# A factorization-machine kernel with attention: the order of its first loads, one gather source for all rows, and later places for transposes, grams and masks

## The chip, the cores and the metric

One core of a Trainium2 chip runs the kernel. The metric is the time of one execution on the device in microseconds; the time before is the median of three runs. Engines are TensorE (PE), VectorE (DVE), ScalarE (ACT), GpSimd (POOL) and SyncE (SP). SP and ACT each feed a DMA queue of their own, and GpSimd feeds a third one.

## The reference

For each of 2048 batch elements, 32 integer indices pick 32 rows of an embedding table (12500 x 64, fp32). Every pair of the 32 rows is multiplied element by element, put through a small attention layer, and summed with the attention score as weight.

```
V = emb_v[x]                                  # (32, 2048, 64); x is brought into 0..12499
iu, ju = np.triu_indices(32, k=1)             # 496 pairs
VV = V[iu] * V[ju]
hid = relu(einsum('pbk,kh->pbh', VV, at_w) + at_b)
score = einsum('pbh,ho->pbo', hid, at_h)
at_fm_score = sum(VV * score, axis=0) @ p
logit = at_fm_score + w0 + sum(w1[x], axis=0)
prob = sigmoid(logit)
```

Since p is applied after the sum over pairs, `VV @ p` of a pair (i, j) is an entry of a weighted Gram matrix of the 32 rows of one batch element. The kernel computes that matrix ("gram"), computes the scores of all pairs, and multiplies the two.

## The kernel before

The batch is cut into 32 **fills** of 64 elements each. A fill's rows come by 16 indirect DMAs of 128 rows each, issued by GpSimd (`gather`, L262), into one of two buffers `rows`. On PE, eight transposes (`turn`, L504) put them into a slot of the PSUM tensor `Z`; ACT copies them to `V` (`keep_v`, L418), scales them by p in two halves (`keep_pv`, L427) and copies the w1 column out (`keep_w1`, L438). A fill then has 16 **rounds** (`ORDER`). In a round, DVE makes products of pairs, `X` (L409); PE multiplies them by `at_w` into `Z` (`hidden`, L536); ACT applies bias and relu, giving `H` (L489). `X` and `H` have four slots of two rounds each, `Z` has three slots of one round, and the transposes take a turn of one of the three. After rounds 3, 7, 11 and 15 PE computes the scores of two steps (`scores`, L553), those after round 3 for the fill before. `grams` (L570) is 128 small matmuls. DVE masks a gram (`mask_gram`), multiplies it by the scores (`weigh`) and sums the pairs (`sum_pairs`).

Each engine's order is written out by hand. Before the change, the transposes of fill t+1 stand ahead of round 8 of fill t, and the grams of fill t+1 stand at the end of fill t. Fill 0 and the last fill are written out; the 30 between are a hardware loop of 15 turns, two fills in each (`over_fills`, L199). The end of a turn is thus the end of every second fill, where each engine jumps back.

**The joint table.** A gathered row should bring its w1 value along. So the kernel first builds a table in DRAM with 66 values a row: it loads the whole embedding table in four pieces of 768 KB (`load_piece`, two on SP's queue, two on ACT's) and w1; DVE and ACT copy both into `joined`, and `store_piece` writes it back. The last 212 rows go through `tail` and `tail_w1`. Gathers from the table wait until everything of it is stored (L286). To start sooner, the eight gathers of the first half of fill 0 read the raw embedding table instead, and eight more at the very end fetch their w1 values (L302). DVE brings the indices into range first (L313 to L321). Small operands (p, bias, hcol, at_w in two halves each, w0) are loaded through SP's queue between the table's loads and its stores.

Gathers of fill t from 4 on are paced by waits on PE's progress: on `scored`, and on `z_ready` by `GROUP_AFTER`.

## Time and profile before

| what | us |
|---|---|
| median of 3 runs | 851.7 |
| lowest, highest run | 846.13, 852.37 |
| profiled execution, its own time | 846.66 |
| its span in the profile | 844.6 |
| PE busy in the span | 785.1 |
| DVE, ACT, POOL busy | 701.3, 648.1, 549.0 |

The span runs from the first to the last recorded instruction; the execution's own time is 2.06 us longer. Busy is the time in which an engine had an instruction running; waits and the issuing of DMAs by SP and ACT are not in it. The chain that ended last is followed back from the last instruction to whatever released each step, so its shares say where the end was decided.

### The profile page before, as it was taken

The page shows a single profiled execution, that of the slowest core. Times are in us where ns is not written, and L with a number is a line of the kernel's source. Part 1 is how long each engine was busy: PE and PEld are TensorE (multiplying, and loading weights), DVE is VectorE, ACT ScalarE, POOL GpSimd, SP SyncE. Part 2 cuts the span into 40 slices and gives each one's busy share as a digit, 9 for nine tenths or more (in the row PEclk, how much of TensorE's full clock was granted, in tenths as well). Part 3 has the DMA queues.
Part 4 walks back from the last instruction along what each step waited for, and adds up shares of the span by engine and source line. Part 5 has one row for each costly group of instructions (what it writes and reads, how often), then busy time and mean ns, then how long its engine had stood idle before and what let it go on. Part 6 is the DMA issues. An engine that isn't in the chain of part 4 may idle for free.

```text
span 844.6 us, 30455 instructions
## 1 busy us (share of the span) xinstructions
PE 785.1 (93%) x12600; PEld 336.8 (40%) x12600; DVE 701.3 (83%) x1181; ACT 648.1 (77%) x679; POOL 549.0 (65%) x530
## 2 busy tenths in 40 slices
PE   0368799999999999999999999999999999999998
PEld 0123344444434444444344444434444444344443
DVE  3367788889988888899888889998888899888883
ACT  2256577878888788888878888887878788887885
POOL 4377776666677666666776666667766666767500
PEclk9979899999999999999999999999999999999999
DMA  7458887532424436333233436352322436323100
GB/s 238 107 26 26 25 25 26 22 22 22 22 23 23 21 21 23 21 22 23 22 23 22 22 21 22 22 25 20 23 22 21 22 21 23 24 20 23 9 1 2
DMA packets 19138, 24.20 MB, mean 29 GB/s; under 512 B 9705, under 2 KB 9774, under 8 KB 19118
## 3 DMA queue, kind: packets, MB, share of 16 engines
q0 software_dynamic: 16640, 17.07, 39.5%
q1 hardware_dynamic: 1703, 3.61, 1.1%
q10 hardware_dynamic: 774, 3.25, 1.0%
q8 instruction: 13, 0.21, 0.1%
q14 instruction: 8, 0.06, 0.0%
HBM read 20.59 MB, written 3.31 MB: 28 GB/s over the span
## 4 chain that ended last, share of the span: by engine, by line
PE 83%; POOL 4%; issue 4%; DVE 3%; DMA 3%; SPq 2%; ACT 0%; DVEq 0%; POOLq 0%
PE Z L549 50%; PE SG L564 26%; POOL rows L276 4%; PE SG L579 4%; PE Z L513 4%; DVE X L409 3%; DMA table<-joined 1%; DMA rows<-table,joint_idx 1%; SPq L236 1%; PE Z L634 0%; SPq L237 0%; SPq L229 0%; SPq L239 0%; SPq L238 0%; DVE part L384 0%
## 5 line engine op out<-in xcount | busy, mean ns | idle before, releaser
L276 POOL DMA_INDIRECT rows<-table,joint_idx x504 | 531.0, 1054 | 233.9 <-issue 144.9
L409 DVE TENSOR_TENSOR X<-V 128x992 f32<-128x992 f32 (+15 forms) x1024 | 635.9, 692 | 40.9 <-PE Z L549 22.0
L489 ACT ACTIVATE H<-Z,bias 128x1024 f32<-128x1024 f32 x512 | 536.6, 1118 | 112.5 <-PE Z L549 109.2
L549 PE MATMUL Z<-X,w_sb 64*64 64x512 f32 x4096 | 473.6, 598 | 9.2 <-issue 5.1
L549 PEld LDWEIGHTS Z<-X,w_sb 64*64 64x64 f32 x4096 | 153.0, 133 | 242.4 <-issue 237.4
L564 PE MATMUL SG<-H,score_w 128*32 128x496 f32 (+15 forms) x4096 | 248.4, 382 | 0.0
L564 PEld LDWEIGHTS SG<-H,score_w 128*32 128x32 f32 x4096 | 109.4, 110 | 204.0 <-issue 109.5
L435 ACT ACTIVATE pV<-V,pmask 128x1024 f32<-128x1024 f32 x64 | 81.0, 1269 | 0.1
L378 DVE TENSOR_TENSOR prod<-SG,gram 128x496 f32<-128x496 f32 x32 | 21.6, 674 | 67.5 <-PE SG L564 67.5
L424 ACT COPY V<-Z 128x1024 f32<-128x1024 f32 x31 | 31.4, 1014 | 43.0 <-PE Z L513 43.0
L579 PE MATMUL SG<-V,pV 128*32 128x32 f32 x4096 | 43.7, 198 | 3.2 <-ACT pV L435 1.6
L579 PEld LDWEIGHTS SG<-V,pV 128*32 128x32 f32 x4096 | 43.1, 109 | 7.1 <-issue 3.8
L513 PE MATMUL Z<-ident,rows 128*128 128x128 f32 x248 | 34.7, 284 | 5.8 <-DMA rows<-table,joint_idx 5.8
L525 PE MATMUL SG<-ident,rows 128*128 128x128 f32 x8 | 2.2, 428 | 38.7 <-DMA rows<-in_L_rec_emb_v_dram,idx 29.9
L513 PEld LDWEIGHTS Z<-ident,rows 128*128 128x128 f32 x248 | 27.3, 143 | 8.7 <-DMA rows<-table,joint_idx 5.0
L370 DVE TENSOR_TENSOR gram<-SG,upper 128x496 f32<-128x496 f32 x32 | 21.6, 675 | 9.8 <-PE SG L579 8.2
L384 DVE TENSOR_REDUCE part<-prod 128x496 f32 (+1 forms) x32 | 21.1, 660 | 0.0
L525 PEld LDWEIGHTS SG<-ident,rows 128*128 128x128 f32 x8 | 1.4, 216 | 39.5 <-issue 29.9
L276 POOL DMA_INDIRECT rows<-in_L_rec_emb_v_dram,idx x8 | 9.3, 1168 | 10.4 <-DVE idx L317 8.3
L358 DVE COPY score_w<-hcol 64x1 f32<-64x1 f32 x32 | 2.2, 150 | 10.3 <-DMA w_sb<-in_L_rec_w_dram 10.3
L443 ACT COPY w_all<-rows 128x8 f32 (+2 forms) x64 | 10.4, 227 | 0.0
L463 ACT COPY V<-SG 128x512 f32<-128x512 f32 x2 | 1.2, 587 | 12.1 <-PE SG L525 12.1
(42 smaller groups left out, 31.9 us busy)
## 6 DMA issues: line engine op xcount, KB each, us to landing
rows<-table,joint_idx POOLq DMA_INDIRECT x504, 3.7
table<-joined ACTq DMA_DIRECT2D x2, 792.0 KB
table<-joined SPq DMA_DIRECT2D x2, 792.0 KB
raw<-in_L_rec_emb_v_dram ACTq DMA_DIRECT2D x2, 768.0 KB, 6.7
raw<-in_L_rec_emb_v_dram SPq DMA_DIRECT2D x2, 768.0 KB, 9.1
idx_raw<-in_r_x_dram SPq DMA_DIRECT2D x4, 64.0 KB, 5.9
rows<-in_L_rec_emb_v_dram,idx POOLq DMA_INDIRECT x8, 6.6
w_all<-in_L_rec_w_dram,idx POOLq DMA_INDIRECT x8
```

The source lines that it names most:

```text
L276: pool.indirect_dma_start(out=rows[t % 2][:, g * FILL_M + m, half, c0:c1], out_offset=None, in_=source, in_offset=bass.IndirectOffsetOnAxi ...
L370: nc.vector.tensor_tensor(gram[parity][:, :, 1:FIELDS], SG[parity][:, :, 1:FIELDS], upper[:, 1:FIELDS].unsqueeze(1).to_broadcast(shape), A ...
L378: nc.vector.tensor_tensor(prod[:, :, 1:FIELDS], SG[parity][:, :, 1:FIELDS], gram[parity][:, :, 1:FIELDS], ALU.mult).then_inc(prod_ready, 1)
L384: nc.vector.tensor_reduce(part[:, bass.ds(t * GROUP, GROUP)], prod[:, :, 1:FIELDS], AX.X, ALU.add).then_inc(part_ready, 1)
L409: last_one = nc.vector.tensor_tensor(xo, vj, vi.unsqueeze(3).to_broadcast(shape), ALU.mult)
L424: nc.scalar.copy(V[parity][:, :, :], Z[:, TURN_SLOT, :, :].rearrange("p g (b f) -> p (g b) f", f=FIELDS)).then_inc(v_ready, 1)
L435: nc.scalar.activation(pV[:, :, half, :, :], V[parity][:, :, :].rearrange("p b (i c) -> p b c i", c=2), ACT.Copy, scale=pmask[:, half:half ...
L489: nc.scalar.activation(H[:, s % H_SLOTS, :, COLS * g:COLS * g + COLS], Z[:, z_slot(r), :, :], ACT.Relu, bias=bias[:, 0:1]).then_inc(hid_re ...
L513: last = nc.tensor.transpose(Z[:, TURN_SLOT, g, 128 * m:128 * m + 128], embs[:, g * FILL_M + m, 1:1 + 2 * EMB], ident[:, :])
L549: done = nc.tensor.matmul(Z[64 * par:64 * par + 64, z_slot(r), half, :], w_sb[k, :], X[k, s % X_SLOTS, par, COLS * g:COLS * g + COLS], sta ...
L564: last = nc.tensor.matmul(SG[parity][at:at + 32, :, j0:FIELDS], score_w[:, slot, :], hid.rearrange("p (b j) -> p b j", j=nj), start=(s == ...
L579: last = nc.tensor.matmul(SG[parity][at:at + 32, b, :], pV[:, g * GROUP + b, half, :, :].rearrange("p c i -> p (c i)"), V[parity][:, g * G ...
```

## The change

Nine things are altered:
- SP loads its two table pieces ahead of the indices; ACT loads w1 ahead of its two pieces.
- The tail's rows, the tail of w1 and all nine small loads are issued by GpSimd, which also joins the tail (two copies) and stores it.
- DVE joins w1 and its two table pieces ahead of the work on the indices.
- All 16 gathers of fill 0 read the joint table and wait for it. The early gathers from the raw table, the zeroing of their w1 column, and the eight w1 gathers at the end are gone.
- The transposes of the next fill stand ahead of round 12 instead of 8; ACT's copy to `V` moves with them, and `keep_w1` is ahead of round 14.
- `grams(t)` stands in its own fill t, behind the scores after round 3; ACT makes its two `pV` halves ahead of rounds 0 and 2 of that fill.
- DVE masks ahead of round 10, weighs ahead of 11, sums ahead of 13 (before: 8, 10, 12).
- The gathers' pacing waits are later: `scored` by two steps, `GROUP_AFTER` (0, 6, 10, 13).
- `turn(1)` keeps its old slot of `Z` by a name of its own.

```diff
@@ -43,13 +43,15 @@
-TURN_BEFORE = 8
+TURN_BEFORE = 12
+PV_BEFORE = (0, 2)
+MASKED_BEFORE, WEIGHED_BEFORE, SUMMED_BEFORE = 10, 11, 13
 SCORED_AFTER = {3: (-1, (6, 7)), 7: (0, (0, 1)), 11: (0, (2, 3)), 15: (0, (4, 5))}
 LAST_STEPS = (6, 7)
 X_SLOTS, H_SLOTS, Z_SLOTS = 4, 4, 3
 ROW = EMB + 1
-EMB_AT, W1_AT = (1, 0), (0, EMB)
+W1_AT = (0, EMB)
 JOINT = EMB + 2
@@ -57,7 +59,7 @@
 TAIL = (VOCAB - MAIN) // TAIL_RUN
-GROUP_AFTER = (0, 3, 7, 10)
+GROUP_AFTER = (0, 6, 10, 13)
@@ -71,7 +73,7 @@
-TURN_SLOT = TURN_BEFORE % Z_SLOTS
+TURN_SLOT, FIRST_TURN_SLOT = TURN_BEFORE % Z_SLOTS, Z_SLOTS - 1
@@ -225,22 +227,12 @@
+            for k in range(PIECES // 2):
+                load_piece(sp, k)
             for q in range(QUARTERS):
                 sp.dma_start(idx_raw[q * FIELDS:(q + 1) * FIELDS, :],
                              r_x[:, q * NB:(q + 1) * NB]).then_inc(idx_loaded, 16)
-            for k in range(PIECES // 2):
-                load_piece(sp, k)
-            sp.dma_start(tail[:, :, 1:1 + EMB], last_rows(emb_v)).then_inc(tail_loaded, 16)
-            for half in range(2):
-                lo, hi = half * 64, half * 64 + 64
-                sp.dma_start(pcol[lo:hi, :], p).then_inc(small_loaded, 16)
-                sp.dma_start(bias[lo:hi, :], at_b.rearrange("(h o) -> h o", o=1)).then_inc(small_loaded, 16)
-                sp.dma_start(hcol[lo:hi, :], at_h).then_inc(small_loaded, 16)
-                sp.dma_start(w_sb[lo:hi, :], at_w).then_inc(small_loaded, 16)
-            sp.dma_start(w0_sb[:, :], w0.to_broadcast([QUARTERS, 1])).then_inc(small_loaded, 16)
-            sp.wait_ge(w1_joined, 4)
-            sp.wait_ge(tail_loaded, 16)
-            sp.dma_start(last_rows(table), tail[:, :, :]).then_inc(table_stored, 16)
+            sp.wait_ge(w1_joined, 2)
             for k in range(PIECES // 2):
@@ -264,27 +256,34 @@
                         if paced and g == 0 and m == 0:
-                            pool.wait_ge(scored, STEPS * (t - 3) + LAST_STEPS[0] - 1)
+                            pool.wait_ge(scored, STEPS * (t - 3) + LAST_STEPS[0] + 1)
                         elif paced and m % 2 == 0:
                             pool.wait_ge(z_ready, ROUNDS * (t - 2) + GROUP_AFTER[2 * g + m // 2])
-                        joint = t > 0 or g > 0
-                        source, at_rows = (flat, joint_idx) if joint else (emb_v, idx)
                         for half in range(2):
                             col = (2 * half + g) * NM + t * FILL_M + m
-                            c0, c1 = (0, ROW) if joint else (EMB_AT[half], EMB_AT[half] + EMB)
                             arrived = first_rows[g] if t == 0 else second_rows if t == 1 else rows_gathered[t % 2]
-                            pool.indirect_dma_start(out=rows[t % 2][:, g * FILL_M + m, half, c0:c1], out_offset=None,
-                                                    in_=source,
-                                                    in_offset=bass.IndirectOffsetOnAxis(ap=at_rows[:, col:col + 1], axis=0)
+                            pool.indirect_dma_start(out=rows[t % 2][:, g * FILL_M + m, half, :], out_offset=None, in_=flat,
+                                                    in_offset=bass.IndirectOffsetOnAxis(ap=joint_idx[:, col:col + 1], axis=0)
                                                     ).then_inc(arrived, 16)
+            pool.dma_start(tail[:, :, 1:1 + EMB], last_rows(emb_v)).then_inc(tail_loaded, 16)
+            pool.dma_start(tail_w1[:, :], w1[MAIN:VOCAB, :].rearrange("(p r) o -> p (r o)", r=TAIL_RUN)).then_inc(tail_loaded, 16)
             for half in range(2):
-                nc.gpsimd.memset(rows[0][:, 0:FILL_M, half, W1_AT[half]], 0.0).then_inc(w1_cleared, 1)
-            pool.wait_ge(idx_ready, 1)
-            gather(0, groups=(0,))
+                lo, hi = half * 64, half * 64 + 64
+                pool.dma_start(hcol[lo:hi, :], at_h).then_inc(small_loaded, 16)
+                pool.dma_start(pcol[lo:hi, :], p).then_inc(small_loaded, 16)
+                pool.dma_start(bias[lo:hi, :], at_b.rearrange("(h o) -> h o", o=1)).then_inc(small_loaded, 16)
+                pool.dma_start(w_sb[lo:hi, :], at_w).then_inc(small_loaded, 16)
+            pool.dma_start(w0_sb[:, :], w0.to_broadcast([QUARTERS, 1])).then_inc(small_loaded, 16)
+            pool.wait_ge(tail_loaded, 32)
+            for c in (0, 1 + EMB):
+                nc.gpsimd.tensor_copy(tail[:, :, c], tail_w1[:, :]).then_inc(tail_joined, 1)
+            pool.wait_ge(tail_joined, 2)
+            pool.dma_start(last_rows(table), tail[:, :, :]).then_inc(tail_stored, 16)
             pool.wait_ge(idx_ready, 4)
-            pool.wait_ge(table_stored, 16 * (PIECES + 1))
-            gather(0, groups=(1,))
+            pool.wait_ge(table_stored, 16 * PIECES)
+            pool.wait_ge(tail_stored, 16)
+            gather(0)
             gather(1)
@@ -296,16 +295,18 @@
                 gather(t, paced=True)
-            for half in range(2):
-                for n in range(FILL_M):
-                    at = bass.IndirectOffsetOnAxis(ap=idx[:, 2 * half * NM + n:2 * half * NM + n + 1], axis=0)
-                    pool.indirect_dma_start(out=w1_all[:, 2 * half, n:n + 1], out_offset=None, in_=w1, in_offset=at
-                                            ).then_inc(w1_first, 16)
         @block.vector
         def _(dve):
+            dve.wait_ge(w1_loaded, 16)
+            for c in (0, 1 + EMB):
+                nc.vector.tensor_copy(joined[:, :, c], raw_w1[:, :]).then_inc(w1_joined, 1)
+            for k in range(PIECES // 2):
+                dve.wait_ge(raw_loaded[k], 16)
+                r0, r1 = k * PIECE, (k + 1) * PIECE
+                nc.vector.tensor_copy(joined[:, r0:r1, 1:1 + EMB], raw[:, r0:r1, :]).then_inc(rows_joined[k], 1)
             dve.wait_ge(idx_loaded, 16 * QUARTERS)
@@ -390,11 +383,11 @@
                         dve.wait_ge(first_v, g + 1)
-                    if r == 8:
+                    if r == MASKED_BEFORE:
                         mask_gram(t, parity)
-                    if r == 10 and not first:
+                    if r == WEIGHED_BEFORE and not first:
                         weigh(t - 1, 1 - parity)
-                    if r == 12 and not first:
+                    if r == SUMMED_BEFORE and not first:
                         sum_pairs(t - 1)
@@ -421,7 +414,8 @@
                     act.wait_ge(gram_ready, t - 1)
-                nc.scalar.copy(V[parity][:, :, :], Z[:, TURN_SLOT, :, :].rearrange("p g (b f) -> p (g b) f", f=FIELDS)
+                slot = FIRST_TURN_SLOT if isinstance(t, int) and t == 1 else TURN_SLOT
+                nc.scalar.copy(V[parity][:, :, :], Z[:, slot, :, :].rearrange("p g (b f) -> p (g b) f", f=FIELDS)
                                ).then_inc(v_ready, 1)
@@ -437,17 +431,15 @@
-                g0 = 1 if isinstance(t, int) and t == 0 else 0
                 for half in range(2):
-                    src = rows[parity][:, :, half, W1_AT[half]].rearrange("p (g m) -> p g m", g=2)[:, g0:2, :]
-                    nc.scalar.copy(w1_all[:, 2 * half + g0:2 * half + 2, bass.ds(t * FILL_M, FILL_M)], src
+                    src = rows[parity][:, :, half, W1_AT[half]].rearrange("p (g m) -> p g m", g=2)
+                    nc.scalar.copy(w1_all[:, 2 * half:2 * half + 2, bass.ds(t * FILL_M, FILL_M)], src
                                    ).then_inc(w1_kept, 1)
+            nc.scalar.dma_start(raw_w1[:, :], w1[0:MAIN, :].rearrange("(p r) o -> p (r o)", p=128)).then_inc(w1_loaded, 16)
             for k in range(PIECES // 2, PIECES):
                 load_piece(nc.scalar, k)
-            nc.scalar.dma_start(raw_w1[:, :], w1[0:MAIN, :].rearrange("(p r) o -> p (r o)", p=128)).then_inc(w1_loaded, 16)
-            nc.scalar.dma_start(tail_w1[:, :], w1[MAIN:VOCAB, :].rearrange("(p r) o -> p (r o)", r=TAIL_RUN)).then_inc(w1_loaded, 16)
-            act.wait_ge(w1_joined, 3)
+            act.wait_ge(w1_joined, 2)
             for k in range(PIECES // 2, PIECES):
@@ -467,14 +458,12 @@
                     if not last and not first:
-                        if r == 8:
+                        if r == TURN_BEFORE:
                             keep_v(t + 1, 1 - parity)
-                        if r == 10:
-                            keep_pv(t + 1, 1 - parity, 0)
-                        if r == 12:
+                        if r == 14:
                             keep_w1(t + 1, 1 - parity)
-                        if r == 14:
-                            keep_pv(t + 1, 1 - parity, 1)
+                    if not first and r in PV_BEFORE:
+                        keep_pv(t, parity, PV_BEFORE.index(r))
                     if first and r == STEPS // 2:
@@ -490,8 +479,6 @@
                     keep_v(1, 1)
-                    for half in range(2):
-                        keep_pv(1, 1, half)
                     keep_w1(1, 1)
@@ -507,10 +494,11 @@
                     pe.wait_ge(rows_gathered[parity], gathered(t, parity))
+                slot = FIRST_TURN_SLOT if isinstance(t, int) and t == 1 else TURN_SLOT
                 embs = rows[parity][:, :, :, :].rearrange("p t h k -> p t (h k)")
                 for g in range(2):
                     for m in range(FILL_M):
-                        last = nc.tensor.transpose(Z[:, TURN_SLOT, g, 128 * m:128 * m + 128],
+                        last = nc.tensor.transpose(Z[:, slot, g, 128 * m:128 * m + 128],
                                                    embs[:, g * FILL_M + m, 1:1 + 2 * EMB], ident[:, :])
@@ -608,12 +596,11 @@
                                 scores(t - 1, 1 - parity, s)
-                    if r == ROUNDS - 1 and not last:
-                        grams(t + 1, 1 - parity)
+                        if back < 0 and not first:
+                            grams(t, parity)
             def linear_term():
-                pe.wait_ge(w1_first, 16 * 2 * FILL_M)
                 pe.wait_ge(w1_kept, 2 * FILLS)
```

## Rows read from the trace of the kernel before

**Rows 1.** The page: busy time of each engine, its share of the span, instructions.

```profile
PE 785.1 (93%) x12600; PEld 336.8 (40%) x12600; DVE 701.3 (83%) x1181; ACT 648.1 (77%) x679; POOL 549.0 (65%) x530
```

**Rows 2.** Waits of the PE from 120 to 800 us: total, times, longest.

```profile
PE Z L549 <- issue: 5.1, 12, 0.5
PE Z L549 <- DVE X L409: 0.8, 2, 0.4
```

**Rows 3.** Timeline of the PE, two boundaries between fills: start, us, line, idle before.

```profile
156.97 1.31 PE L579 MATMUL SG<-V,pV 128*32 128x32 f32 x128
158.32 3.66 PE L549 MATMUL Z<-X,w_sb 64*64 64x512 f32 x32
...
179.35 1.94 PE L564 MATMUL SG<-H,score_w 128*32 128x368 f32 x32
181.10 1.31 PE L579 MATMUL SG<-V,pV 128*32 128x32 f32 x128
182.83 2.38 PE L549 MATMUL Z<-X,w_sb 64*64 64x512 f32 x20 [0.42 <-issue]
```

**Rows 4.** Timeline of the start, all engines and queues: start, us, line, idle before.

```profile
4.77 8.67 SPq L236 DMA_DIRECT2D pcol<-in_L_rec_p_dram  x1
...
12.94 0.26 DVE L327 COPY joined<-raw_w 128x96 f32<-128x96 f32 x1 [1.05 <-DMA tail_w<-in_L_rec_w_dram]
...
27.49 2.17 DVE L358 COPY score_w<-hcol 64x1 f32<-64x1 f32 x32 [10.31 <-DMA w_sb<-in_L_rec_w_dram]
```

**Rows 5.** The chain that ended last: start, us, what.

```profile
20.81 11.90 DMA table<-joined
```

**Rows 6.** Busy time by stretch, after the engines: granted clock, DMA share, GB/s.

```profile
22.00:24.00 2.00, 0.00 (x0) 0.00 (x0) 0.00 (x0) 0.00 (x0) 0.00 (x0) 1.00 0.75 63
...
26.00:28.00 2.00, 0.00 (x0) 0.00 (x0) 0.51 (x9) 0.20 (x1) 0.00 (x0) 1.00 0.96 362
```

**Rows 7.** Timeline of GpSimd: one early gather, then the 8th and 40th from the table.

```profile
12.81 2.45 POOL L276 DMA_INDIRECT rows<-in_L_rec_emb_v_dram,idx  x1 [0.30 <-issue]
...
42.74 0.94 POOL L276 DMA_INDIRECT rows<-table,joint_idx  x1 [0.30 <-issue]
...
83.92 0.95 POOL L276 DMA_INDIRECT rows<-table,joint_idx  x1 [0.30 <-issue]
```

**Rows 8.** Timeline of the PE, first, second and third fill.

```profile
29.89 1.08 PE L525 MATMUL SG<-ident,rows 128*128 128x128 f32 x4 [29.89 <-DMA rows<-in_L_rec_emb_v_dram,idx]
...
46.56 1.11 PE L525 MATMUL SG<-ident,rows 128*128 128x128 f32 x4 [8.76 <-DMA rows<-table,joint_idx]
...
69.16 1.07 PE L513 MATMUL Z<-ident,rows 128*128 128x128 f32 x8 [0.96 <-DMA rows<-table,joint_idx]
...
93.34 1.97 PE L513 MATMUL Z<-ident,rows 128*128 128x128 f32 x8 [4.86 <-DMA rows<-table,joint_idx]
95.24 4.83 PE L549 MATMUL Z<-X,w_sb 64*64 64x512 f32 x32
...
108.65 0.96 PE L579 MATMUL SG<-V,pV 128*32 128x32 f32 x64 [0.68 <-issue]
109.65 3.66 PE L549 MATMUL Z<-X,w_sb 64*64 64x512 f32 x32
```

**Rows 9.** Timeline of ScalarE in the third fill.

```profile
121.73 1.01 ACT L424 COPY V<-Z 128x1024 f32<-128x1024 f32 x1 [1.25 <-PE Z L513]
122.86 2.12 ACT L489 ACTIVATE H<-Z,bias 128x1024 f32<-128x1024 f32 x2
124.87 1.28 ACT L435 ACTIVATE pV<-V,pmask 128x1024 f32<-128x1024 f32 x1
```

**Rows 10.** The page: groups of products, of weighing and of w1 copies: count, busy, mean ns.

```profile
L409 DVE TENSOR_TENSOR X<-V 128x992 f32<-128x992 f32 (+15 forms) x1024 | 635.9, 692 | 40.9 <-PE Z L549 22.0
...
L378 DVE TENSOR_TENSOR prod<-SG,gram 128x496 f32<-128x496 f32 x32 | 21.6, 674 | 67.5 <-PE SG L564 67.5
...
L443 ACT COPY w_all<-rows 128x8 f32 (+2 forms) x64 | 10.4, 227 | 0.0
```

More of the change, by code:

```diff
@@ L163, in afm_kernel @@
         w1_joined = sem("w1_joined")
-        w1_cleared = sem("w1_cleared")
+        tail_joined = sem("tail_joined")
+        tail_stored = sem("tail_stored")
         table_stored = sem("table_stored")
@@ L173, in afm_kernel @@
         ident_ready = sem("ident_ready")
-        w1_first = sem("w1_first")
         first_rows = [sem(f"first_rows{g}") for g in range(2)]
@@ L322, in _ @@
                                         ).then_inc(idx_ready, 1)
-            dve.wait_ge(w1_loaded, 32)
-            for c in (0, 1 + EMB):
-                nc.vector.tensor_copy(joined[:, :, c], raw_w1[:, :]).then_inc(w1_joined, 1)
-                nc.vector.tensor_copy(tail[:, :, c], tail_w1[:, :]).then_inc(w1_joined, 1)
-            for k in range(PIECES // 2):
-                dve.wait_ge(raw_loaded[k], 16)
-                r0, r1 = k * PIECE, (k + 1) * PIECE
-                nc.vector.tensor_copy(joined[:, r0:r1, 1:1 + EMB], raw[:, r0:r1, :]).then_inc(rows_joined[k], 1)
             nc.vector.memset(zeros[:, :], 0.0)
@@ L457, in _ @@
             act.wait_ge(small_loaded, 16 * 9)
-            act.wait_ge(w1_cleared, 2)
             nc.scalar.activation(warm[:, :], w0_sb[:, :], ACT.Sigmoid).then_inc(sigmoid_loaded, 1)
```

## The prediction, made before the kernel with the change had run

> **What bounds it now.** I read the page's busy shares first: PE is busy 93% of the span, and no other engine is above 83% [rows 1]. Then the waits of PE between 120 and 800 us: 5.1 us in 12 gaps of kind "issue" and 0.8 in two more [rows 2]. In 680 us that is all, so from the third fill on PE sets the time, and work moved about on DVE, ACT or GpSimd is worth nothing there unless it makes PE wait. The timeline of PE shows where those gaps sit: at a boundary inside a loop turn, grams end at 158.28 and the next products follow at 158.32; where the loop jumps back, grams end at 182.41 and products start at 182.83 [rows 3]. Fills 1 to 30 are 15 turns, hence 14 jumps: 14 x 0.42 = 5.9 us.
>
> The rest of PE's idle time is at the start. First transposes 29.89, second group 46.56, those of fill 1 69.16, those of fill 2 93.34, products of fill 2 109.65 [rows 8]; three of the four ended a wait for gathered rows. The gathers waited for the table, whose last stores landed at 20.81 + 11.90 = 32.7 [rows 5]. I call that moment T.
>
> **Edit 1: the table earlier.** Before, SP's queue was held 8.67 us in issuing pcol and free at 13.44; w1, behind ACT's two pieces, reached DVE at 12.94 [rows 4]. So the loads end near 13, and they carry the same bytes after. What falls away is the time between 13 and 20.8, in which SP issued small loads. Pieces 0 and 2 will have landed early and be joined by then. Four stores of 792 KB are 3.24 MB; at 362 GB/s [rows 6] that is 9.0 us, so T is 22.0 at best. Before, the last two stores took 11.9 us for bytes worth 4.5, behind small loads that held the DMA engines at 0.75 share for 63 GB/s [rows 6]. At worst they do so again: 13 + 4.5 + 11.9 = 29.4. The small loads still use the same engines, only from another queue, earlier. I take 2.5 us for them: T = 24.5, nearer the lower end since the queue ahead of the stores is now empty.
>
> The tail goes through GpSimd: 11 loads, two copies, one store. No row shows a plain DMA from GpSimd. The nearest is a gather: from the 8th to the 40th, (83.92 - 42.74)/32 = 1.29 us each [rows 7]. From about 2: 11 x 1.29 = 14.2, copies at most 0.5, store 1.3, landing 2.9 (8th gather issued by 43.68, its rows used at 46.56). That is 21. One gather beside DVE's copies into the table took 2.45 instead of 0.94 [rows 7]; twice that excess gives 24, still under T. Lower end: an issue of 0.6, T unaffected. Upper end: every one at 2.45 + 0.3, T = 2 + 30.3 + 4.7 = 37. I take 1.29.
>
> Small operands were ready at 27.49 + 2.17 = 29.7 [rows 4] and bounded the first transposes; now those come at T + 13.8 = 38.3, which covers the loads, the index work after DVE's joins (under 3 us) and the constants. If that cover goes, they cost what they end beyond 38.3.
>
> **Edit 2: 48 gathers in one row.** Before, rows were there at T + 13.8 (8 gathers), T + 36.4 (24), T + 60.6 (40): (93.34 - 46.56)/32 = 1.46 us each, slower than their issue. Kept at 1.46: 16 gathers T + 25.5, 32 T + 48.9, 48 T + 72.3. Losing the early eight costs 8 x 1.46 = 11.7 us; that is the price of the single source. The eight w1 gathers at the end were on nobody's path: nothing.
>
> **Edit 3: what fill 1 does while it waits.** PE reached the transposes of fill 2 after eight rounds, waited 4.86 us, and still had eight rounds and the grams to do. After, it has twelve rounds done. From the transposes of fill 1: V 2.1, first X 1.25 (DVE needs 635.9/512 = 1.24 a round [rows 10]), four rounds at DVE's pace to 8.2, scores to 10.1, grams 1.3 plus a first-time gap of 0.68 [rows 8] to 12.1, four rounds 15.8, scores 17.7, four rounds 21.4, scores 23.3: T + 72.2. Rows come at T + 72.3, so PE hardly waits. Then transposes 1.0, four rounds 3.66, scores 1.94: fill 2 starts at T + 78.9. Its grams (1.3) now lie within it, so T + 80.2 stands against 109.65. The head gives T - 29.4; at T = 24.5 that is **-4.9 us**. Break-even is T = 29.4.
>
> **Edit 4: the loop's jump.** Ahead of the jump stood 128 grams in 1.31 us, 10 ns for a matmul with its weight load. Now it is 32 score matmuls in 1.94 us, 60 ns each [rows 3]. Whatever PE's sequencer has run ahead by is worth six times as much time. Gain between 0 and 5.9; I take all, as grams at 10 ns a pair were fed without a hole, so the queue should be full under scores. The Trainium skill, Advanced Engine Details and Errata, section Engine Queue Depths, gives TensorE a queue of 64; by it the scores cover nearly their whole 1.94 us. No run here shows the depth.
>
> **Edit 5: steady rounds.** Take a fill's first products as 0. Transposes end at -5.5, V is copied by -4.5 (1.01 [rows 9]). DVE then starts 4.5 us ahead instead of eight rounds ahead: X(3) at +0.5, wanted at 2.7; ten rounds, then the mask (0.67) end at 8.6, wanted by scores at 10.5. Slack 1.9. ACT: relus of 12 and 13 -4.4 to -2.3, w1 copies 2 x 0.23 [rows 10], relus 14 and 15 to +0.1, pV 1.28, relu 0 to 2.4; `hidden(3)` needs its slot at 2.75. Slack 0.35, and 0.4 for `hidden(15)`. The same pattern stands before around round 8, with 0.45 and no gap in PE. Cost nothing; the cover is that slack. GpSimd's pacing is later, but a fill's last gather is issued near 25 and used at 42. Nothing.
>
> **Sum.** 846.66 (profiled execution; span 844.6 and 2.06 around) - 4.9 - 5.9 = 835.9. The median of the runs stands 5.0 above that execution, which no view explains; I carry it: **841 us**.
>
> **Rivals.**
> A, the forecast: 841, own range 837 to 846 (T 22 to 26, jump 4 to 5.9). Chance 0.48.
> B, the jump isn't covered: the 0.42 is the jump itself and stays, behind scores. For it: it is there each time, to 0.05 us. Against: no gap like it behind grams elsewhere. 851.7 - 4.9 = 846.8. Chance 0.18.
> C, GpSimd's queue gives T: its 11 loads are late or held by DVE's copies, the small operands with them. For: the gather of 2.45. Against: DVE copies for a few us only. At T = 33: 851.7 + 3.6 - 5.9 = 849.4; at 37, 853.4. It decides from T = 24.5 on. The Trainium skill, SBUF — State Buffer, section SBUF: two separate sides, says that an fp32 copy on DVE locks GpSimd out while it writes descriptors; the 2.45 us agrees. Chance 0.14.
> D, slower: ACT becomes the bound. pV ahead of rounds 0 and 2 and V ahead of 12 push the relus, and PE waits for a `Z` slot at `hidden(3)` and `hidden(15)`. It decides once semaphores take more than the 0.35 of slack; at 0.35 beyond, 2 x 29 x 0.35 = 20.3: 851.7 - 10.8 + 20.3 = 861. For: the thinnest slack of all. Against: round 8 before. Chance 0.10, a third of it under 1% slower.
> E, the head gives more: T = 20 to 22 and faster gathers, since nothing else shares the queues: 851.7 - 8.4 - 5.9 = 837. Chance 0.10.
>
> **Numbers.** Faster by over 1% is below 843.2 (1% is what a measurement of this kernel can tell from no change). It holds in E and in four fifths of A: 0.48. Slower by over 1%: most of D, 0.08. Between: 0.44. The range leaves out D and the ends of C and E: 836 to 852.
>
> **What would show it.** Right: the first gather issued near 25; transposes of fill 0 near 38 and 50, of fill 2 near 97 with no wait above 1 us; no 0.42 gap each 48 us; two fills in 48.2 us instead of 48.6. Edit 1 is wrong if the first gather comes after 29; edit 3 if PE waits there for rows; edit 4 if the gap stays; edit 5 if PE waits for ACT or DVE inside fills. The forecast as a whole fails if T passes 29 or a wait comes back in every fill.

## The result, and the profile after

The changed kernel takes 857.31 us in the median of 20 runs (851.6 to 866.89), the kernel before 852.36 in the same number (843.28 to 854.0, and one of 2042.3). The ratio is 1.0064 with a 95% interval of 1.0041 to 1.0086: some 5 us slower, where 10 us faster was forecast. The profiled execution of the changed kernel took 866.18 us, 9 above its median. It is one of three slow runs among the 20, and the one before, 846.66, lies 5.7 below its median, so the spans of the two traces, 864.2 and 844.6 us, are 19.6 apart where the medians are 5 apart. I measure gains and losses between these two spans; how the 5 us of the medians divide, no trace shows.

The page after, for [rows 1, 10]: gathers are L265 now and grams L567.

```profile
PE 799.7 (93%) x12600; PEld 343.6 (40%) x12600; DVE 694.3 (80%) x1179; ACT 648.1 (75%) x679; POOL 641.8 (74%) x534
...
L265 POOL DMA_INDIRECT rows<-table,joint_idx x512 | 630.7, 1232 | 170.6 <-issue 150.7
...
L567 PE MATMUL SG<-V,pV 128*32 128x32 f32 x4096 | 58.1, 200 | 4.8 <-issue 1.4
```

PE is busy 14.6 us longer (before 785.1) with the same 12600 matmuls. The grams alone are busy 58.1 us; the same group had 43.7 on the page before. A gather takes 1232 ns in the mean, not 1054.

The waits of PE from 130 to 830 us, for [rows 2]: the gaps of kind "issue" are gone, and a wait for gathered rows has come in.

```profile
PE Z L501 <- DMA rows<-table,joint_idx: 11.5, 5, 4.1
```

The start, for [rows 4, 5]:

```profile
5.13 0.57 POOL L273 DMA_DIRECT2D hcol<-in_L_rec_at_h_dram  x1
...
7.45 3.74 SPq L225 DMA_DIRECT2D table<-joined  x2
...
22.95 2.17 DVE L351 COPY score_w<-hcol 64x1 f32<-64x1 f32 x32 [2.65 <-DMA w_sb<-in_L_rec_w_dram]
24.68 1.05 POOL L265 DMA_INDIRECT rows<-table,joint_idx  x1 [6.47 <-DMA table<-joined]
```

SP issues its first store at 7.45, small operands are ready at 22.95 + 2.17, and the first gather stands at 24.68, when the last piece has landed at 23.8. T is thus 24 and not 32.7. The tail's store, issued by GpSimd at 17.66, landed at 23.6, only 0.2 us ahead of that last piece. PE's start, for [rows 8]:

```profile
37.63 1.09 PE L513 MATMUL SG<-ident,rows 128*128 128x128 f32 x4 [37.63 <-DMA rows<-table,joint_idx]
...
48.42 1.11 PE L513 MATMUL SG<-ident,rows 128*128 128x128 f32 x4 [2.83 <-DMA rows<-table,joint_idx]
...
70.73 1.06 PE L501 MATMUL Z<-ident,rows 128*128 128x128 f32 x8 [0.38 <-DMA rows<-table,joint_idx]
...
86.73 1.94 PE L537 MATMUL Z<-X,w_sb 64*64 64x512 f32 x14 [1.26 <-issue]
...
95.96 1.09 PE L501 MATMUL Z<-ident,rows 128*128 128x128 f32 x8
...
122.16 1.09 PE L501 MATMUL Z<-ident,rows 128*128 128x128 f32 x8
```

The first transposes come at 37.63, the second at 48.42, fill 1's at 70.73, fill 2's at 95.96 with no wait, fill 3's at 122.16. Before, fill 3's stood at 120.60, but four rounds and one group of scores earlier in the order. At the same state of the work, with these transposes, those rounds and the scores done, the kernel before stands at 127.08 and the changed one at 123.18: 3.9 us ahead. The gap of kind "issue" (one more of 1.40 stands at 110.98) is in PE's first pass through the loop's code.

PE's timeline in the steady fills, for [rows 3]. The loop jumps back at 227.2.

```profile
225.33 1.94 PE L552 MATMUL SG<-H,score_w 128*32 128x368 f32 x32
227.19 3.66 PE L537 MATMUL Z<-X,w_sb 64*64 64x512 f32 x32
...
232.54 1.96 PE L567 MATMUL SG<-V,pV 128*32 128x32 f32 x128
```

At the jump nothing is lost. But grams take 1.96 us here, and over 1.5 in 23 of the 27 fills between 130 and 800 us (mostly 1.9 to 2.1). Before, one of 28 was over 1.5 and the rest took 1.30 to 1.32. GpSimd's timeline before shows what stood beside such a group, the one of 156.97 in [rows 3]:

```profile
153.32 0.95 POOL L276 DMA_INDIRECT rows<-table,joint_idx  x1 [0.30 <-issue]
157.10 1.98 POOL L276 DMA_INDIRECT rows<-table,joint_idx  x1 [2.83 <-PE SG L564]
```

In all 27 groups of fills 3 to 29, a gather began 0.13 us into the grams and took 1.59 to 1.98 us instead of 0.95: I call such a gather held. The one slow group of fill 30 (1.89) had two gathers of 0.95 beside it.

### The profile page after: what moved, and what is told of

Read it like the earlier page. It is cut to its first block, busy times and chain, and to the rows that moved or that the text cites. A ratio compares the mean times of both kernels' runs of the same rounds, so it can differ in the third digit from the quotient of the medians.

```text
span 864.2 us, 30460 instructions
## 1 busy us (share of the span) xinstructions
PE 799.7 (93%) x12600; PEld 343.6 (40%) x12600; DVE 694.3 (80%) x1179; ACT 648.1 (75%) x679; POOL 641.8 (74%) x534
## 4 chain that ended last, share of the span: by engine, by line
PE 85%; DMA 6%; POOL 5%; issue 2%; ACT 1%; DVE 0%; ACTq 0%; DVEq 0%; POOLq 0%
PE Z L537 50%; PE SG L552 25%; PE SG L567 6%; POOL rows L265 5%; PE Z L501 4%; DMA rows<-table,joint_idx 3%; DMA raw<-in_L_rec_emb_v_dram 2%; DMA table<-joined 1%; ACT H L478 1%; PE Z L621 0%; DVE X L402 0%; ACT joined L446 0%; PE SG L513 0%; ACT V L418 0%; PE Z L609 0%
## 5 line engine op out<-in xcount | busy, mean ns | idle before, releaser
L265 POOL DMA_INDIRECT rows<-table,joint_idx x512 | 630.7, 1232 | 170.6 <-issue 150.7
L537 PEld LDWEIGHTS Z<-X,w_sb 64*64 64x64 f32 x4096 | 151.2, 133 | 233.4 <-issue 226.0
L567 PE MATMUL SG<-V,pV 128*32 128x32 f32 x4096 | 58.1, 200 | 4.8 <-issue 1.4
L567 PEld LDWEIGHTS SG<-V,pV 128*32 128x32 f32 x4096 | 51.6, 110 | 17.7 <-issue 11.8
L501 PE MATMUL Z<-ident,rows 128*128 128x128 f32 x248 | 34.7, 284 | 11.9 <-DMA rows<-table,joint_idx 11.9
L436 ACT COPY w_all<-rows 128x8 f32 (+1 forms) x64 | 9.8, 208 | 0.0
```

The source lines that it names most:

```text
L265: pool.indirect_dma_start(out=rows[t % 2][:, g * FILL_M + m, half, :], out_offset=None, in_=flat, in_offset=bass.IndirectOffsetOnAxis(ap=j ...
L501: last = nc.tensor.transpose(Z[:, slot, g, 128 * m:128 * m + 128], embs[:, g * FILL_M + m, 1:1 + 2 * EMB], ident[:, :])
L537: done = nc.tensor.matmul(Z[64 * par:64 * par + 64, z_slot(r), half, :], w_sb[k, :], X[k, s % X_SLOTS, par, COLS * g:COLS * g + COLS], sta ...
L567: last = nc.tensor.matmul(SG[parity][at:at + 32, b, :], pV[:, g * GROUP + b, half, :, :].rearrange("p c i -> p (c i)"), V[parity][:, g * G ...
```

## The experiments

The theory at the outset (S): the loss sits in the steady fills. Grams now lie where GpSimd is issuing gathers, which stretches them; and gathers themselves are held up, so that rows come late. Rivals: H, the head costs it; P, the new place in PE's program is the cause and the gathers are not; Q, the later pacing alone; D, long gathers come from a full DMA queue. From e7 on, L stands for the theory that a long gather is held by DVE's unbroken products. These letters are not those of the prediction's rivals. In the lists below a fill's time is the distance from one group of transposes to the next, in the mean over 24 fills of the steady part, and the number of long gathers (over 3 us) is counted between 130 and 790 us.

**e1, head alone.** Constants and orders of the steady part set back (ACT's `pV` and w1 copies too, not shown):

```diff
-TURN_BEFORE = 12
+TURN_BEFORE = 8
-MASKED_BEFORE, WEIGHED_BEFORE, SUMMED_BEFORE = 10, 11, 13
+MASKED_BEFORE, WEIGHED_BEFORE, SUMMED_BEFORE = 8, 10, 12
-GROUP_AFTER = (0, 6, 10, 13)
+GROUP_AFTER = (0, 3, 7, 10)
-                            pool.wait_ge(scored, STEPS * (t - 3) + LAST_STEPS[0] + 1)
+                            pool.wait_ge(scored, STEPS * (t - 3) + LAST_STEPS[0] - 1)
...
+                    if r == ROUNDS - 1 and not last:
+                        grams(t + 1, 1 - parity)
```

> Head edits alone (first loads, GpSimd's small loads, one joint table for all rows); transposes at round 8, grams at the end of the fill, masks and pacing as before. Theory S (the loss sits in the steady fills: grams beside running gathers, and gathers held up): here steady fills go as before, two fills in 48.6 us, grams 1.31 us each. Only the head differs: transposes of fill 2 near T + 72 = 96, wait there some 7 us, fill 2 begins near 112.5 instead of 109.7, so +3 us: near 855. Rival H (the head costs the time, for instance GpSimd's queue or the table): as slow as the whole change or slower, 857 and up, with T above 29.

Measured: 853.72 against 852.21 of the kernel before, ratio 1.0033 (0.9994 to 1.0072). The first gather came at 24.60, the transposes of fill 2 at 95.7 after a wait of 4.7 us, those of fill 3 at 123.0 instead of 120.6. So the early table does not pay by itself: eight more gathers in the row take back what it gives. H falls. But the steady fills of this trace don't go quite as before: 24.66 us a fill. One gather took 14.73 us and PE waited 3.18 us for its rows at 346.02, and 5 of 28 groups of grams took 1.85 to 1.94.

**e2, steady part alone.** The converse edit on the kernel before, its head kept: the steady part of the diff above, and nothing of its first loads.

> The head as before (early gathers from the raw table, old order of loads); transposes at round 12, grams in their own fill, masks and pacing as changed. Theory S: the jump's gap of 0.42 us is gone (-5.9), the wait before the transposes of fill 2 shrinks (about -8 against before), grams take 2.1 us in most fills and some transposes wait for rows (+16 as in the changed kernel): near 854. Rival H: steady fills are no slower, so 852.4 - 5.9 - 8 = 838 to 843.

Measured: 853.71 against 852.21, ratio 1.0009 (0.998 to 1.0037). 24.79 us a fill instead of 24.32, grams 2.04 in the mean, 24 long gathers. The steady part is slower. The total is not accounted for. The transposes of fill 2 wait no more, but two gaps of kind "issue" of 3.49 and 2.77 us in fills 1 and 2 take more than that gives: at the state of the work in which the changed kernel was 3.9 us ahead, this one is 2.5 us behind (transposes of fill 3 at 128.54). Its profiled execution took 860.84 us, 7 more than its median.

**e3 and e4, no gathers in the loop.** The same edit on the changed kernel (e3) and on the one before (e4): fills from 4 on are not gathered and compute on the rows of fills 2 and 3, so only the loop is read.

```diff
-            for t in range(4, FILLS):
-                pool.wait_ge(rows_turned, t - 2)
-                pool.wait_ge(w1_kept, 2 * (t - 1))
-                gather(t, paced=True)
...
-                else:
-                    pe.wait_ge(rows_gathered[parity], gathered(t, parity))
...
+                if first:
+                    pe.wait_ge(rows_gathered[0], 16 * GATHERS)
+                    pe.wait_ge(rows_gathered[1], 16 * GATHERS)
```

> The changed kernel without the gathers of fills 4 to 31 (later fills compute on the rows of fills 2 and 3), PE waits once for fills 2 and 3 ahead of the loop. Read in the loop only. Theory S: with no gathers running, all grams take 1.31 us, no gap at the jump, two fills in 48.2 us. Rival P (place in PE's program: grams so soon behind the jump are short of instructions or ready data): grams stay at 1.9 to 2.1 us.

> The kernel before without the gathers of fills 4 to 31, PE waits once ahead of the loop. Read in the loop only. Both theories: grams 1.31 us. The gap of 0.42 at the jump: it stays if it belongs to the jump behind grams (then two fills in 48.6), and is gone if it is an effect of the gathers (48.2).

PE's timeline of e3; the loop jumps back at 501.9:

```profile
500.05 1.94 PE L546 MATMUL SG<-H,score_w 128*32 128x368 f32 x32
501.91 3.66 PE L531 MATMUL Z<-X,w_sb 64*64 64x512 f32 x32
...
507.26 1.30 PE L561 MATMUL SG<-V,pV 128*32 128x32 f32 x128
```

and of e4, with the jump at 504.3:

```profile
502.98 1.30 PE L573 MATMUL SG<-V,pV 128*32 128x32 f32 x128
504.70 3.66 PE L543 MATMUL Z<-X,w_sb 64*64 64x512 f32 x32 [0.42 <-issue]
```

Without gathers the changed kernel's grams take 1.30 and a fill 24.03 us. The kernel before keeps its 0.42 at the jump and takes 24.32. P falls: in the same place of the program, behind the same instructions, grams are fast once no gather runs. Edit 4 of the prediction holds: the gap is gone. The two kernels differ by 0.28 us a fill here; 0.42 for every second fill is 0.21 of it, and no view puts a name to the other 0.07. With gathers the changed kernel needs 25.2 us a fill in the mean and mostly 24.65 to 24.86, over 0.6 more than without, where the kernel before needs nothing more (24.32 with and without).

**e8, DMA traffic without GpSimd.** e3 with 420 copies of 128 table rows, issued by SyncE:

```diff
+            sp.wait_ge(rows_gathered[1], 16 * GATHERS)
+            for n in range(420):
+                v0 = 128 * (n % 90)
+                sp.dma_start(scratch[:, n % 2, :], table[v0:v0 + 128, 0:ROW]).then_inc(copied[n % 2], 16)
+                if n > 0:
+                    sp.wait_ge(copied[(n - 1) % 2], 16 * ((n - 1) // 2 + 1))
```

> The changed kernel without the gathers of fills 4 to 31, as before, but SyncE copies 128 table rows (260 bytes each) into an unused buffer 420 times, two in flight, while the loop runs. Read in the loop only. If it is DMA traffic into SBUF that stretches the grams, they take 1.9 to 2.1 us here too. If it is what GpSimd itself does in issuing a gather, they stay at 1.30.

Busy time of a stretch with the copies (last columns: granted clock, DMA share, GB/s), and one group of grams:

```profile
300.00:324.00 24.00, 24.00 (x396) 10.36 (x392) 21.10 (x36) 20.00 (x22) 0.00 (x0) 1.00 0.22 39
```

```profile
414.56 1.30 PE L570 MATMUL SG<-V,pV 128*32 128x32 f32 x128
```

39 GB/s, more than the gathers' 22, and the grams stay at 1.30 in the 14 fills (3 to 16) beside which the copies ran, with 149 to 288 packets starting during each. In the changed kernel they were slowed with 33 to 52. So it is not the amount of traffic. Traffic of GpSimd's own queue remains as a rival; e10 and e11 below speak to it.

**e5, e6, e7 on another chip.** Three single edits of the changed kernel: old pacing; the first wait of `gather(t)` put behind the grams; old places of the masks.

```diff
-                            pool.wait_ge(scored, STEPS * (t - 3) + LAST_STEPS[0] + 1)
+                            pool.wait_ge(gram_ready, t - 1)
```

> The changed kernel with the old pacing of the gathers (first wait for scored of step 4, GROUP_AFTER 0, 3, 7, 10). A fill's gathers may start some 5 us earlier. Theory S: grams still lie amid running gathers, 1.9 to 2.1 us; but rows are no longer late, so no transposes wait in the loop; 24.03 + 0.7 = 24.8 us a fill, in all near 852 to 855. Rival Q (only the later pacing costs the time): as forecast first, 841 to 845.

> The changed kernel, the gathers of fill t start only when the grams of fill t-2 are done (one wait replaced). Theory S: wherever GpSimd reaches that wait ahead of the grams, these run beside no gather and take 1.3 to 1.4 us. A fill's 16 gathers take 20.0 us at the usual 1.25, and 24.6 with the long ones seen after the change, against 24.1 of the fill: if the long ones persist, GpSimd is late and only part of the grams is fast. 843 if all fast, 855 if none. Rival P (place in PE's program): grams 2.1 throughout, 857 and up.

> The changed kernel with mask, weighing and summing ahead of rounds 8, 10, 12 of DVE as before. Theory L (a gather that meets DVE's unbroken run of products in rounds 13 to 15 is held until DVE stops, 3.9 us): the run is broken otherwise, since DVE waits at the mask for the grams; the 22 gathers of over 3 us become few, rows are in time, grams stay at 2.0: 852 to 855. Rival D (the long gathers come from the DMA queue being full): they stay, 857.

This chip ran every kernel with gathers in the loop near 1200 us, with a granted clock of 0.87 to 0.89 in the mean of the traces, the kernel before at 1223.43; its times are compared with nothing on other chips. e5: 1231.97, ratio 1.0048 (0.9997 to 1.0099). e6: 1209.51, no interval. e7: 1172.01, ratio 0.9567 (0.9463 to 0.9671). The absolute forecasts are missed for that reason; the traces still tell. The chip is not slow as such: e8 ran on it too, in 898.18 us, and its loop without gathers took 24.04 us a fill at a granted clock of 1.00. In e5, PE's gaps of kind "issue" between 130 and 800 us add up to 112 us, in products and scores as well as in grams; e8 has one, of 1.4. Why gathers cost PE so much more on this chip is open. PE in e7 beside running gathers, then the gathers:

```profile
236.94 0.98 PE L567 MATMUL SG<-V,pV 128*32 128x32 f32 x44
238.39 0.28 PE L567 MATMUL SG<-V,pV 128*32 128x32 f32 x6 [0.48 <-issue]
...
241.38 0.26 PE L567 MATMUL SG<-V,pV 128*32 128x32 f32 x4 [1.20 <-issue]
242.81 1.11 PE L567 MATMUL SG<-V,pV 128*32 128x32 f32 x63 [1.18 <-issue]
```

```profile
237.07 0.95 POOL L265 DMA_INDIRECT rows<-table,joint_idx  x1 [8.27 <-PE SG L552]
...
240.85 0.95 POOL L265 DMA_INDIRECT rows<-table,joint_idx  x1 [0.30 <-issue]
```

Grams that begin while GpSimd issues one gather after the other stop and go: 128 matmuls take 7 us, and run on when the fourth gather is out. In e6 no gather runs beside the grams; PE, then GpSimd, whose next gather waits for them:

```profile
349.06 1.30 PE L567 MATMUL SG<-V,pV 128*32 128x32 f32 x128
```

```profile
339.24 0.95 POOL L265 DMA_INDIRECT rows<-table,joint_idx  x1 [0.30 <-issue]
351.14 1.52 POOL L265 DMA_INDIRECT rows<-table,joint_idx  x1 [10.96 <-PE SG L567]
```

1.30 us in all fills from 3 on, on the same chip. That is theory S at its clearest. e5 shows it from the other side: gathers that are held leave the grams fast. In 12 fills its grams took 5.6 to 8.5 us with 122 to 198 DMA packets starting meanwhile; in nearly all others 1.30 with none, though in most of these a single gather of 7.1 to 9.2 us was under way all the time. Q is not shown wrong by time here, but its grams are as disturbed as the others'.

**e9, e10, e11 on a chip at the usual speed.** e9 is e6 again, e11 is e7 again, e10 is both edits together:

```diff
-MASKED_BEFORE, WEIGHED_BEFORE, SUMMED_BEFORE = 10, 11, 13
+MASKED_BEFORE, WEIGHED_BEFORE, SUMMED_BEFORE = 8, 10, 12
...
-                            pool.wait_ge(scored, STEPS * (t - 3) + LAST_STEPS[0] + 1)
+                            pool.wait_ge(gram_ready, t - 1)
```

> The kernel of e6_after_grams once more, since the chip of that call ran every kernel near 1220 us. There its grams took 1.30 us in all steady fills, with no gather beside them. Theory S: here too they take 1.3 to 1.4 wherever GpSimd gets to its wait in time; with the long gathers of 3.9 us still there it often does not, so 846 to 853 against 857 of the changed kernel. Rival P: no better than 857.

> The changed kernel, gathers start behind the grams, and DVE's mask, weighing and summing ahead of rounds 8, 10, 12 as before. Theories S and L together: no gather over 3 us, GpSimd done before the next grams, grams 1.30, no gap at the jump, no late rows: 24.05 us a fill, and the head's gain: 852.4 - 8 - 2 = 842, the best of all. Rival D (long gathers come from a full DMA queue): they stay and it is as e9.

> The kernel of e7_old_masks once more, on a chip at its usual speed. Theory L: hardly a gather over 3 us (2 of 297 in that call), no transposes wait for rows in the loop; theory S: grams still 1.9 to 2.1. 24.75 us a fill, 852 to 855. Rival D: 22 long gathers again and 857.

| kernel | median us | before, same chip | ratio | interval | us a fill | grams, mean | long gathers |
|---|---|---|---|---|---|---|---|
| e9 | 855.69 | 853.26 | 1.0034 | 1.0001 to 1.0066 | 24.91 | 2.06 | 22 |
| e11 | 848.96 | 853.26 | 0.9992 | 0.9948 to 1.0037 | 24.50 | 1.71 | 0 |
| e10 | 838.95 | 853.26 | 0.9851 | 0.9792 to 0.991 | 24.09 | 1.37 | 0 |

e9 missed its 846 to 853: the wait for the grams alone helps little, since GpSimd is in time for it in one fill of 28. The reason stands in its timeline, one gather of 3.9 us in most fills:

```profile
513.40 3.88 POOL L265 DMA_INDIRECT rows<-table,joint_idx  x1 [0.30 <-issue]
```

e11 has no long gather and no wait for rows, and came out below its 852 to 855; its grams are still beside gathers and take 1.59 to 1.91. PE, then GpSimd:

```profile
505.53 1.59 PE L567 MATMUL SG<-V,pV 128*32 128x32 f32 x128
```

```profile
505.66 1.07 POOL L265 DMA_INDIRECT rows<-table,joint_idx  x1 [3.74 <-PE SG L552]
```

This is the picture of the kernel before, a pause of GpSimd and then a gather that begins 0.13 us into the grams. But this gather takes 1.07 and not 1.98, and the grams are slow. So in the kernel before it was not the pause that kept them fast; the gather was held. In 15 of e11's slowed groups no DMA packet at all started meanwhile. e11 also keeps the whole later pacing, so the pacing alone makes no rows late. e10 has both edits, and PE's view of waits between 130 and 800 us is empty. PE (the loop jumps at 518.4), then GpSimd:

```profile
499.77 1.30 PE L567 MATMUL SG<-V,pV 128*32 128x32 f32 x128
...
516.59 1.93 PE L552 MATMUL SG<-H,score_w 128*32 128x368 f32 x32
518.46 3.67 PE L537 MATMUL Z<-X,w_sb 64*64 64x512 f32 x32
```

```profile
501.86 1.59 POOL L265 DMA_INDIRECT rows<-table,joint_idx  x1 [1.99 <-PE SG L567]
...
522.93 0.95 POOL L265 DMA_INDIRECT rows<-table,joint_idx  x1 [0.30 <-issue]
525.89 1.59 POOL L265 DMA_INDIRECT rows<-table,joint_idx  x1 [2.00 <-PE SG L567]
```

GpSimd has issued its 16 gathers by 523.88, stands still while the grams run from 523.80, and starts again at 525.89. In 24 of the 28 fills from 3 to 30 the grams take 1.30; in the other four one more gather falls beside them, and they take 1.80. During the 24 groups of 1.30 GpSimd's queue still starts 22.5 packets per us, during the stretched groups of the changed kernel 22.6. So packets of that queue don't slow the grams either, and what is left is the issuing of a gather itself. By which path it reaches PE, no run shows. e10 is 1.5% under the kernel before, with an interval of 0.9 to 2.1%, from four runs.

**e12, what holds a gather.** Back to the changed kernel. A long gather, DVE's products beside it, and the busy times of the stretch, with granted clock, DMA share and GB/s at the end:

```profile
214.96 1.33 POOL L265 DMA_INDIRECT rows<-table,joint_idx  x1 [0.30 <-issue]
216.59 3.89 POOL L265 DMA_INDIRECT rows<-table,joint_idx  x1 [0.30 <-PE Z L537]
```

```profile
215.97 3.69 DVE L402 TENSOR_TENSOR X<-V 128x608 f32<-128x608 f32 x6
```

```profile
214.00:216.50 2.50, 2.50 (x40) 0.97 (x36) 2.50 (x5) 1.13 (x3) 1.99 (x2) 1.00 0.33 20
216.60:220.50 3.90, 3.90 (x52) 1.41 (x48) 3.05 (x6) 3.90 (x4) 3.88 (x1) 1.00 0.09 12
```

DVE's products of rounds 13 to 15 run without a break from 215.97 to 219.66; the gather that begins at 216.59 ends 0.8 us behind them, and the DMA share falls to 0.09, so the queue is not full but nearly empty. All 22 long gathers of the loop end 0.82 to 0.83 us after such a run of DVE, and so does the one of 14.73 us in e1. It isn't so everywhere: most of e5's longest, and the 2 that stay over 3 us in the run below, end while DVE is at work. The edit cuts these products short:

```diff
                     for slot, j0, nj, c0 in segments(s):
+                        if not first and r >= 13:
+                            nj = 1
```

> The changed kernel, with DVE's products of rounds 13, 14 and 15 of each fill but the first cut to 16 elements a partition and half (the rest of those X is left as it was, so the output is another). GpSimd's pacing, the gathers and PE's work are unchanged. Theory L (a gather beside DVE's unbroken products of rounds 13 to 15 is held until DVE stops): no gather over 3 us in the loop, no transposes that wait for rows. Rival D (the queue or the memory holds them): 20 or more over 3 us as before. Theory S: grams still 1.9 to 2.1 in most fills, so about 24.75 us a fill.

Its one run took 851.21 us, one of the kernel before 846.97. GpSimd at the same place of the fill, with the same 1.34 ahead of it:

```profile
512.83 1.34 POOL L265 DMA_INDIRECT rows<-table,joint_idx  x1 [0.30 <-issue]
514.47 1.04 POOL L265 DMA_INDIRECT rows<-table,joint_idx  x1 [0.30 <-issue]
```

2 gathers over 3 us instead of 22, no wait for rows, 24.52 us a fill, grams 1.79. D falls. That the hold depends on DVE's products of these rounds is shown; which of its operations do it, and why the same products in the kernel before (192.1 to 197.0) let gathers through in 0.95 to 1.40 us, is not. In e10 and e11 the same products run too, with the sum ahead of round 12 instead of 13, and hold nothing. So it seems to hang on how the gathers fall among DVE's instructions, which is argued and not shown.

## Why the prediction was wrong

**Edit 1 (T) was right in its number, in part by luck.** T came at 24 for the forecast 24.5. But the last piece was loaded at 15.2 and not 13, and the first store went out at 7.45, beside the loads. Of GpSimd's 11 loads, eight took 0.5 to 0.6 us each to issue, not 1.29 (the others 0.89, 1.26 and 2.45). They landed slowly, the tail of w1 11.9 us after its issue, so the tail's store landed at 23.6, 0.2 us short of deciding T; in e10 it landed at 24.0, behind the last piece (23.9). Rival C was near, by the landing and not by the issue.

**Edits 2 and 3 were right, with two errors that cancel.** Forecast: T + 72.2 for the transposes of fill 2; measured 95.96 - 24 = 72. Fill 1's transposes came at T + 47, 2 us earlier than forecast, and the way from them to fill 2's took 25.2 us and not 23.3. The head gives 3.9 us, forecast 4.9. What was left out are the gaps in PE's first pass (1.26 and 1.40 us after). In e10 they are 3.27 and 1.94, and its transposes of fill 2 come at 100.31, 4 us later. PE in e10:

```profile
89.45 2.80 PE L537 MATMUL Z<-X,w_sb 64*64 64x512 f32 x14 [3.27 <-issue]
```

A 16 KB packet of the queue that the profile calls "instruction" runs from 87.2 to 88.1 us, 1.3 before this gap ends. In the traces of the changed kernel, the kernel before, e1, e2 and e9 to e12, every gap of this kind over 0.5 us in the first pass ends 1.1 to 1.5 us after the end of such a packet. That fits a wait for instructions, but no run tests it.

**Edit 4 was right.** No gap at the jump; worth 14 x 0.42 = 5.9 us, and e3 against e4 gives 0.07 us a fill more, 2.0 in all.

**The steady rounds, edit 5, are the step that failed**, twice. The grams' new place was priced at nothing ("Its grams (1.3) now lie within it", under edit 3, and no term for it under edit 5), and so was the pacing ("GpSimd's pacing is later ... Nothing").
The price of the grams was taken from rows in which the gather beside them was held: 1.59 to 1.98 us instead of 0.95, in every steady fill but one. The warning was in the trace: the groups of fills 0, 1, 2 and 30 had unheld gathers of 0.94 to 1.13 beside them and took 2.00, 2.38, 2.41 and 1.89, and I read fill 2's as a first-time gap alone. The changed kernel runs the grams while gathers go out. One group from 232.54 on, PE's weight loads with what GpSimd does beside them:

```profile
232.77 0.95 POOL L265 DMA_INDIRECT rows<-table,joint_idx  x1 [0.30 <-PE SG L552]
233.40 0.61 PEld L567 LDWEIGHTS SG<-V,pV 128*32 128x32 f32 x57 [0.18 <-issue]
234.03 0.96 POOL L265 DMA_INDIRECT rows<-table,joint_idx  x1 [0.30 <-issue]
234.20 0.19 PEld L567 LDWEIGHTS SG<-V,pV 128*32 128x32 f32 x8 [0.19 <-issue]
```

The weight loads stop twice, for 0.18 and 0.19 us, and run a little slower between. From fill 3 on all grams together take 55.4 us, before 38.5: **+16.9 us**.

The second half: I reckoned that the last gather of a fill is issued long before its use, at 1.29 us each. With one gather of 3.9 us in most fills and several of 1.3 to 1.9, a fill's 16 take 16 x (1.232 + 0.30) = 24.5 us, more than the 24.03 that PE needs. GpSimd falls behind until PE waits for rows: 11.5 us in five waits, and with this comes the clock. What brought the long gathers is the move of mask, weighing and summing, which I had priced by DVE's own slack alone: back in their old places, with the later pacing kept, there is none (e11). At 348.00 the wait is 4.10 us; behind it the granted clock of 348 to 352 is 0.61, that is most of the stretch at 1.2 and not 2.4 GHz, and the transposes take 1.97 instead of 1.09:

```profile
348.00 1.97 PE L501 MATMUL Z<-ident,rows 128*128 128x128 f32 x8 [4.10 <-DMA rows<-table,joint_idx]
349.90 4.24 PE L537 MATMUL Z<-X,w_sb 64*64 64x512 f32 x32
```

The products behind two of the waits take 4.24 and 5.36 instead of 3.66, so with the transposes the low clock costs 3.2 us. The sum for the profiled execution: -3.9 (head) - 5.9 (jump) - 2.0 (e3 against e4) + 16.9 (grams) + 11.5 (waits for rows) + 3.2 (clock) = +19.8, against 19.6 measured in the spans. The last two terms are probably smaller in a run near the median: e9, with the same grams and long gathers, has one such wait, of 2.3 us, and a span of 854.6. No trace of the changed kernel near its median shows it.

Rival D of the prediction (ACT as the bound) did not happen: nowhere in the loop does PE wait for ACT. It had the sign and not the mechanism. The median before, 5 us over its profiled execution, was carried and not explained; that stays so.

That the scores cover the jump agrees with the queue depth of 64 that the Trainium skill gives TensorE (Advanced Engine Details and Errata, section Engine Queue Depths), since nothing is lost there; no run measured the depth. The rule of the Trainium skill on fp32 copies of DVE and GpSimd's descriptor writes (SBUF — State Buffer, section SBUF: two separate sides) was weighed for the start alone. There two small loads beside DVE's copies took 1.26 and 0.89 us to issue instead of 0.52, which agrees, and neither set T. The 3.9 us gathers of the loop are of its kind, but these products are tensor_tensor operations and not the copies it names, so that is only a likeness.

## What to carry to other kernels

Before moving a burst of many short matmuls, look at what GpSimd is doing beside it at the old place and at the new one. At its full pace the burst ran where GpSimd issued nothing (e3, e6, e10) or where its gather was held (the kernel before, e5). A price taken from such rows holds only with that company, so if the burst is moved, the gathers are to be kept off its new place; in e10 one wait did it, once the long gathers were gone (1.5% against the kernel before). And when an engine's work per period comes near the period, price its longest instructions too, not the usual one: here 16 x 1.25 = 20.0 us became 24.5, for a period of 24.0.

## What the hardware showed that I had not expected

- A gather being issued by GpSimd slows a burst of 10 ns matmuls on PE (128 in 1.30 us alone, mostly 1.6 to 2.1 beside gathers), while 39 GB/s of traffic from another queue doesn't. On the chip of e5 to e8 the same burst took 7 us beside gathers, and 1.30 without.
- That chip is slow beside gathers alone: 35 to 36 us a fill with them, 24.04 without, at a granted clock of 1.00.
- A gather that is held leaves the burst alone: before, it took 1.59 to 1.98 us, and the grams beside it 1.30.
- A gather can be held for 3.9 us, until 0.8 us after DVE stops (22 of 22 in the changed kernel's loop), at one place of most fills; a change in the places of three DVE instructions removes it.
- PE's first pass through the loop's code has gaps of 0.6 to 3.8 us that no semaphore explains, in every kernel of the usual speed that has gathers beside it; each ends 1.1 to 1.5 us after a 16 KB packet of the instruction queue. e3 without gathers there has none over 0.3, with the same packets.
